# One drain on GpSimd between the last unit's residual gathers and its wait for row tiles

## The reference

```
x = x + tanh(g_xattn) * attention(layernorm(x), ctx)      # 16 heads of 32, causal mask
x = x + tanh(g_ffn)   * ffn(layernorm(x))

# ffn on the 1600 rows:
route    = sigmoid(x @ router_w)                          # 8 experts
max_ind  = argmax(route);  max_prob = route[max_ind]
out[row] = (silu(x @ gate_w[e]) * (x @ up_w[e])) @ down_w[e] * max_prob     with e = max_ind
```

## Time and profile before

| | us |
|---|---|
| median of 3 runs | 521.25 |
| the three runs | 520.55, 521.25, 525.81 |
| span of the profiled execution, first to last instruction | 519.2 |
| busy: PE, DVE, ACT, POOL | 470.9, 379.3, 309.6, 170.0 |

### The profile page before, as it was taken

How to read it: one execution, slowest core, us unless ns; L and a number is a source line. 1 busy time by engine, 2 the same in 40 slices (tenths; PEclk the granted TensorE clock), 3 DMA queues, 4 the chain that set the end, 5 groups by cost and what they waited for, 6 DMA issues and landing times.

```text
span 519.2 us, 11841 instructions
## 1 busy us (share of the span) xinstructions
PE 470.9 (91%) x3892; PEld 396.5 (76%) x3892; DVE 379.3 (73%) x784; ACT 309.6 (60%) x877; POOL 170.0 (33%) x212
## 2 busy tenths in 40 slices
PE   0996999899989998899999999999999999999890
PEld 0984797679668966678888888898888879898770
DVE  3675667877897368977878777778777787878850
ACT  0567566684678376663566675665756656566630
POOL 4316233553654335454322131221232212320111
PEclk9997899999999989999999999999999999999996
DMA  7600030350032004917577768776786767767511
GB/s 195 199 6 3 32 83 2 97 158 20 1 95 80 15 4 134 279 44 188 168 216 227 224 213 289 203 225 200 225 280 213 222 217 234 245 207 248 187 45 31
DMA packets 59357, 77.26 MB, mean 149 GB/s; under 512 B 5552, under 2 KB 40974, under 8 KB 59324
## 3 DMA queue, kind: packets, MB, share of 16 engines
q1 hardware_dynamic: 54268, 66.92, 42.9%
q0 software_dynamic: 5056, 9.93, 6.3%
HBM read 67.76 MB, written 10.34 MB: 150 GB/s over the span
## 4 chain that ended last, share of the span: by engine, by line
PE 38%; DVE 22%; ACT 13%; issue 12%; DMA 10%; SPq 1%; ACTq 1%; DVEq 1%; POOL 0%; POOLq 0%
DMA staging<-in_L_ffn_gate_w 6%; ACT pr L773 5%; DVE gu_lo L973 5%; ACT wq_hi L722 4%; PE bank L1531 4%; PE bank L1533 3%; PE bank L1532 3%; ACT gu_hi L722 3%; PE bank L1641 3%; DVE qT L1493 3%; PE gate_banks L1628 2%; DVE v L1486 2%; DMA staging<-in_L_xattn_Wq 2%; PE gate_banks L1951 2%; DVE wq_lo L973 2%
## 5 line engine op out<-in xcount | busy, mean ns | idle before, releaser
L973 DVE TENSOR_TENSOR gu_lo<-staging,gu_hi 128x1024 fp32r<-128x1024 f32 x64 | 78.2, 1223 | 18.8 <-ACT gu_hi L722 15.7
L1951 PE MATMUL gate_banks<-x_hl,gu_hi 128*128 128x448 f32 x256 | 83.7, 379 | 1.5 <-DVE gu_lo L973 1.2
L1951 PE MATMUL up_banks<-x_hl,gu_hi 128*128 128x448 f32 x256 | 82.9, 375 | 0.0
L517 POOL TENSOR_TENSOR pn<-pr,inv 100x400 f32<-100x400 f32 x64 | 54.6, 856 | 64.0 <-DVE inv L1238 63.8
L722 ACT ACTIVATE gu_hi<-staging 128x1024 fp32r<-128x1024 f32 x64 | 67.3, 1054 | 8.0 <-DMA staging<-in_L_ffn_gate_w 6.2
L1953 PE MATMUL up_banks<-x_hl,gu_lo 128*128 128x224 f32 x256 | 68.1, 266 | 0.0
L1953 PE MATMUL gate_banks<-x_hl,gu_lo 128*128 128x224 f32 x256 | 68.1, 266 | 0.0
L722 ACT ACTIVATE wkv_hi<-qT 128x448 fp32r<-128x448 f32 x32 | 18.5, 579 | 67.4 <-DVE qT L1493 67.4
L1531 PE MATMUL bank<-wq_hi,wkv_hi 128*112 128x512 f32 x128 | 50.8, 397 | 5.1 <-DVE xn L1508 4.2
L1951 PEld LDWEIGHTS gate_banks<-x_hl,gu_hi 128*128 128x128 f32 x256 | 48.1, 188 | 8.0 <-issue 3.1
L773 ACT ACTIVATE pr<-gate_banks,nmx 100x100 f32<-100x100 f32 x128 | 42.2, 354 | 16.6 <-DVE nmx L1232 16.4
(11 more groups left out here) (261 smaller groups left out, 1121.5 us busy)
## 6 DMA issues: line engine op xcount, KB each, us to landing
staging<-in_L_ffn_gate_w SPq DMA_DIRECT2D x32, 512.0 KB, 5.6
staging<-in_L_ffn_up_w SPq DMA_DIRECT2D x32, 512.0 KB
staging<-in_L_ffn_down_w SPq DMA_DIRECT2D x32, 512.0 KB
x_rows<-x SPq DMA_DIRECT2D x8, 800.0 KB
xt<-in_x SPq DMA_DIRECT2D x4, 800.0 KB
xr<-in_x SPq DMA_DIRECT2D x16, 200.0 KB
staging<-in_L_xattn_Wq SPq DMA_DIRECT2D x1, 1024.0 KB, 10.6
x<-in_L_xattn_Wout SPq DMA_DIRECT2D x1, 1024.0 KB, 9.1
```

The lines of the kernel that those rows point to most:

```text
L517: nc.gpsimd.tensor_tensor(pn[0:S, n % DEEP], pr[0:S, n % 2], inv[0:S, n % HP].unsqueeze(2).to_broadcast([S, HP, S]), ALU.mult).then_inc(pr ...
L973: return nc.vector.tensor_tensor(dst, src, hi.bitcast(F32), ALU.subtract)
L1951: nc.tensor.matmul(pair[:, m, 0:2 * CAP], gu_hi[:, s, w, k, r], x_hl[:, :, k, 0:CAP], start=k == 0, stop=False, skip_group_check=True)
```

## The change

Between the issue of the last unit's two residual gathers and the first wait of `send_rows(last)`, GpSimd executes one drain. It carries no semaphore and stands behind the loop, so it is executed once.

```diff
@@ -712,6 +712,7 @@
             send_rows(last - 1)
             wait_sent(last - 1)
             gather_now(first_slot(last), last)
+            pool.drain()
             send_rows(last)
             wait_sent(last)
 
```

## The result

The changed kernel took 514.66 us in the median of six runs (510.37 to 519.3), the kernel before beside it 521.17 us. The ratio is 0.9857, interval 0.9819 to 0.9895: faster by 1.4%, between 1.05% and 1.81%. All ratios and intervals here leave out executions in a disturbed, slower state: one of the changed kernel (519.3 us), one of e8_x60_drain (526.07) and two of e4_end (916.19 and 1153.83). The forecast was 514.5 us, a ratio of 0.987. The mechanism came out as forecast; the low end of the range did not hold: 0.9857 of the 521.25 us that the forecast started from is 513.8 us, 0.1 us under it. The miss is small against the spread, since the plain median of 514.66 us lies inside the range.

The account below looks back on a forecast made before the run. The prediction took GpSimd's 7.09 us closing drain as the kernel's last wait; walking its entries earlier under cover gains 6.75 us, so 521.25 - 6.75 = 514.5 us, range 513.9 to 522.1.

Parts of the forecast that it names:

- The mechanism: Before the first last-unit scatter, the new drain walks the transfer backlog under cover, shortening the closing drain; chance 0.60.
- the low end: Bottom of the forecast range: a closing drain of nearly nothing, 514.16 us, and 0.3 us of scatter, 513.9 us.
- The closing drain is the last wait and pays for a list: End of block: GpSimd's 7.09 us drain walks 86 transfer entries at 0.08 us each.
- fixed price: Rival: any drain behind transfers costs 7.09 us; hidden shares 0.28 with last-transfer and profiler cases, exposed 0.06.
- 84 entries, 6.75 us plus 0.18 us, begun early: New drain behind the last two gathers: starts at 497.86 without awaiting their landing, ends at 504.8, cost 0.
- VectorE's two-operand instructions may stop the walk: During the new drain: 2.48 us of SBUF instructions could make it 0.7 us late, 2.8 with the late start.
- The cover: Between the last gather and GpSimd's wait for `xn`: 8.74 us idle, leaving the new drain 1.8 us to spare.
- Closing drain 0.34 us, gain 6.75 us: End of block: two entries remain, so the closing drain takes 0.34 us in place of 7.09.
- Engine-idle rule: Rival: drains only wait for engine idle; new one gone by 497.9, closing one stays, time unchanged; no separate chance.
- 0.3 us of scatter: Allowance for spread of runs, taken off 514.16 us to set the range's bottom at 513.9 us.
- Chances: For the whole kernel's time: faster 0.60, same 0.34, slower 0.06.
- a price only under the profiler: Rival: closing drain is long only while the profiler writes records, plain runs stay 521.25 us; within a shared 0.28.

Follow-up runs that it names:

- e8_x60_drain: Kernel before plus 60 transfers of 8 bytes on GpSimd and the drain at the change's place; ratio to the kernel before 0.9954.
- e4_end: Kernel before with the one added drain behind `wait_sent(last)`, behind everything; ratio to the kernel before 0.9996.
- e1: Kernel before with one drain only, right behind the first three table transfers; ratio to the kernel before 1.0008.
- e2: Kernel before with one drain only, before the loop over units, behind 31 transfers; ratio to the kernel before 0.9946.
- e9: Kernel before with one drain between the last scatters and the wait for their landing; ratio to the kernel before 0.9965.
- e10: The change plus a second drain one unit earlier, before `send_rows(last - 1)`; ratio to the kernel before 0.9859.
- e3: Kernel before with a drain in each of the six loop turns and at the change's place; ratio to the kernel before 0.9861.

## Why the prediction was right, and where it was wrong

- *The closing drain is the last wait and pays for a list.* Right. Six closing drains lie within 0.02 us of one line, 0.04 us + 0.082 us per transfer: 0 entries 0.040, 2 entries 0.219, 55 entries 4.547, 83 entries 6.846, 86 entries 7.094, 110 entries 9.054. I had guessed between this and a fixed price; e1 and e2 decide it.
- *84 entries, 6.75 us plus 0.18 us, begun early.* Right for this kernel: 7.0 us from the end of the second gather. The reason given, "a walk over closed transfers need not wait for two open ones", holds for half of the walk. e9 shows that the first half runs beside the flight (7.1 us for 86 entries), and e10's earlier drain and e3's first show that the second half waits for the last landing (3.28 us behind it with 79 entries, 1.65 with 39). In the change this added nothing (7.0 us measured, 6.93 by the count): the queue's last packet lies before 497.5, 4.8 us before the end of the drain, and half of the walk is 3.5 us.
- *VectorE's two-operand instructions may stop the walk.* They do not measurably: 7.0 us for 84 entries beside 2.49 us of them (the three rows that end the section on the result), 7.09 us for 86 at the end beside nothing. What they did hold up, by its timing, is the gather before the drain. The contention that the Trainium skill describes in SBUF — State Buffer, section Who interferes with whom, for GpSimd instructions that read SBUF does not reach this walk.
- *The cover.* Right in kind and nearly too small: 0.6 us were left, not 1.8, since the second gather took 1.86 us in place of 1.00.
- *Closing drain 0.34 us, gain 6.75 us.* It is 0.219, since I had taken the start's 0.18 us for a fixed part that is really 0.04; the gain is 6.88 us. That makes 514.4 us of the 514.5, and the last 0.6 us down to the 513.8 of the ratio lie inside its interval.
- *Engine-idle rule.* The new drain's count runs from the end of the engine's last instruction (492.5 to 495.30 is the wait for it). That agrees with the Trainium skill, PSUM — Partial Sum Buffer, section Engine vs sequencer instructions, by which a drain waits for the engine to go idle. But that rule by itself would have left the closing drain at 7.09 us, and it fell to 0.22.
- *The low end: "521.25 - 7.09 = 514.16, and 0.3 us of scatter, 513.9".* This is the step that failed, by the size of its second term. The 7.09 us bound the gain well, but 0.3 us was no measure of the scatter of runs: the prediction names no row for it, and the three runs that it had lie 5.3 us apart (520.55 to 525.81). The changed kernel's runs, without the one of 519.3, spread over 4.8 us, 29 runs of the kernel before over 7.4 us (516.56 to 524.0) and the two profiles differ by 3.7 us upstream. The interval of the ratio, 0.9819 to 0.9895, is 511.8 to 515.8 us on 521.25. A low end of 512 would have been the consistent one.
- *Chances.* The cases of a fixed price and of a price only under the profiler are refuted: e2's, e3's and the change's plain runs moved as their profiles say.

## What to carry to other kernels

Read the sequencers' drains at the end of the block, not only the engines' busy rows: the chain of waits stopped 9 us before the end of the span here, and the 7 us in it were in no table of busy times. Where GpSimd has issued many transfers, put one plain drain where it waits anyway, late enough that few transfers follow and early enough that the drain ends before the awaited work does; then check in the new trace that the next instruction is still released by that work and not by "issue". If transfers are in flight when the drain begins, allow half of its walk behind their landing. Take the spread for a range from the upstream part of the trace and from more than three runs.

## What the runs showed that I had not expected

A drain on GpSimd costs 0.082 us for every transfer that it has issued since its last drain, whether the transfer moves 8 bytes or 230 KB, and long after all of them have landed (7.09 us for 86, in three kernels the same to the nanosecond). It also waits for the landing of transfers in flight, and half of its price, 0.041 us per transfer, comes behind that landing: 0.38 us with 8 transfers, 3.28 with 79. So drains were 6.4 us long with three transfers at the start (e1) and 7.7 to 9.1 us in the loop (e3). And the count has a limit: with 146 transfers 10.4 us, with 170 only 4.0 us. What closes entries there is open.
